# One-hots of the edge sums from a device-memory table, and the bias row of both tiles written by VectorE

## What is computed

```python
edge_feat = jnp.concatenate([x[src], x[dst], edge_attr], axis=-1)
h = mish(edge_feat @ W1 + b1)
messages = mish(h @ W2 + b2)
agg = jax.ops.segment_sum(messages, dst, num_segments=x.shape[0])
```

## Time and profile before

| | |
|---|---|
| median of 3 runs | 1096.25 us (1095.99 to 1096.29) |
| the profiled execution | 1095.75 us |
| its span | 1093.9 us |
| granted TensorE clock, mean | 0.989 |

### The profile page before, as it was taken

The page is one execution under the profiler, slowest core; times in us unless marked ns, Lnnn a source line. Parts: engine busy times, 40 slices in busy tenths (PEclk is TensorE's granted clock), DMA queues, the critical chain, the costliest instruction groups (busy, mean ns, idle before and its releaser), DMA issues.

```text
span 1093.9 us, 18566 instructions
## 1 busy us (share of the span) xinstructions
PE 1037.2 (95%) x5633; PEld 873.0 (80%) x5634; DVE 864.4 (79%) x1500; ACT 886.2 (81%) x1081; POOL 717.4 (66%) x622
## 2 busy tenths in 40 slices
PE   3668999999999999999999999999999999999997
PEld 1226889998889878888888888888888888888796
DVE  7998536635526389999999999999999999999686
ACT  6985735624603699999999999999999999999584
POOL 6874448553255587777777777777777777760227
PEclk9969999999999999999999999999999999999999
DMA  2006962773165387776666676666666666661002
GB/s 106 9 1 151 173 217 93 247 228 116 71 227 119 86 187 161 161 166 136 139 143 146 136 142 145 139 139 138 148 139 138 143 147 134 140 135 39 1 1 95
DMA packets 82914, 141.63 MB, mean 129 GB/s; under 512 B 11115, under 2 KB 39020, under 8 KB 82742
## 3 DMA queue, kind: packets, MB, share of 16 engines
q0 software_dynamic: 38048, 87.58, 39.8%
q1 hardware_dynamic: 44822, 53.52, 15.3%
HBM read 115.42 MB, written 20.39 MB: 124 GB/s over the span
## 4 chain that ended last, share of the span: by engine, by line
PE 85%; DVE 7%; ACT 3%; issue 2%; POOL 1%; DVEq 1%; DMA 1%; ACTq 0%; POOLq 0%
PE banks L1124 12%; PE banks L1125 12%; PE banks L1129 12%; PE banks L1023 9%; PE banks L1156 7%; PE banks L1106 7%; PE banks L1099 6%; PE banks L1066 5%; PE banks L941 4%; PE banks L1087 4%; DVE edge_counts L1799 2%; PE banks L1219 2%; DVE key_onehot L1738 1%; PE banks L996 1%; PE banks L1122 1%
## 5 line engine op out<-in xcount | busy, mean ns | idle before, releaser
L774 POOL DMA_INDIRECT gather_pq<-q_table,dst x157 | 325.2, 2071 | 57.1 <-issue 47.5
L766 POOL DMA_INDIRECT gather_pq<-p_table,src x157 | 174.9, 1114 | 118.6 <-PE banks L1106 67.6
L1124 PE MATMUL banks<-w_lo,h_hi 128*128 128x512 f32 x620 | 242.0, 390 | 0.0
L1125 PE MATMUL banks<-w_hi,h_hi 128*128 128x512 f32 x620 | 241.7, 390 | 0.0
L1129 PE MATMUL banks<-w_hi,h_lo 128*128 128x512 f32 x620 | 166.1, 390 | 0.0
L1129 PEld LDWEIGHTS banks<-w_hi,h_lo 128*128 128x128 f32 x620 | 116.4, 188 | 24.4
L1125 PEld LDWEIGHTS banks<-w_hi,h_hi 128*128 128x128 f32 x620 | 116.4, 188 | 23.7
L1124 PEld LDWEIGHTS banks<-w_lo,h_hi 128*128 128x128 f32 x620 | 116.4, 188 | 23.5 <-issue 0.8
L2107 DVE SCALAR_TENSOR_TENSOR h_full<-mish_work,banks 128x512 f32<-128x512 f32 (+1 forms) x154 | 98.4, 680 | 45.0 <-ACT mish_work L1443 41.2
L2132 DVE SCALAR_TENSOR_TENSOR message<-mish_work,banks 128x1024 f32<-128x1024 f32 x78 | 95.3, 1221 | 8.4 <-ACT mish_work L1467 0.3
L1099 PE MATMUL banks<-ident,gather_pq 128*128 128x128 f32 x628 | 96.5, 275 | 1.5 <-DVE h_full L2107 0.9
(11 more groups left out here) (268 smaller groups left out, 2610.6 us busy)
## 6 DMA issues: line engine op xcount, KB each, us to landing
edge_attr<-in_edge_attr_t SPq DMA_DIRECT2D x20, 256.0 KB, 2.9
attr_high<-edge_attr_hi SPq DMA_DIRECT2D x40, 128.0 KB, 2.1
attr_low<-edge_attr_lo SPq DMA_DIRECT2D x40, 128.0 KB, 1.8
edge_attr_parts<-attr_high SPq DMA_DIRECT2D x79, 64.0 KB, 2.8
edge_attr_parts<-attr_low SPq DMA_DIRECT2D x79, 64.0 KB, 3.7
x_nodes<-h_hi POOLq DMA_DIRECT2D x10, 256.0 KB, 15.0
x_nodes<-h_lo POOLq DMA_DIRECT2D x10, 256.0 KB, 7.8
p_table<-p_stage SPq DMA_DIRECT2D x10, 256.0 KB, 2.0
```

The source lines that it names most:

```text
L766: nc.gpsimd.indirect_dma_start(GP[:, 2 * j + k, :], None, p_tab[:, :], bass.IndirectOffsetOnAxis(ap=SRC[:, 2 * s + k:2 * s + k + 1], axis= ...
L774: nc.gpsimd.indirect_dma_start(GP[:, 2 * j + k, :], None, q_tab[:, :], bass.IndirectOffsetOnAxis(ap=DST[:, 2 * s + k:2 * s + k + 1], axis= ...
L1124: pe.matmul(at, h_high(s, j)[:, c, e], W2_LO[:, c, :], start=False, stop=False, skip_group_check=True)
L1125: pe.matmul(at, h_high(s, j)[:, c, e], W2_HI[:, c, :], start=False, stop=False, skip_group_check=True)
```

## The change

- The one-hots of the sums are no longer made in the loop. `four_hots` on DVE makes those of four edge tiles (one 128x512 comparison) in places ahead of the loop: 22 between the statistics of the first product, 7 in those of the second, 10 behind the rows of Q; `store_hots` on ACT issues a 256 KB store of each into a table in device memory. The two buffers lie in the unused part of `iota`, and POOL writes that part anew before the loop.
- In the loop SP loads the one-hots of one step at a time (128 KB), behind the attributes of a later step (`further_hots`), and PE waits for them ahead of the sums.
- DVE writes the bias row of both tiles with one copy (`b2_both_tiles`) behind each message. ACT's copy and PE's matmul with ones are gone for all steps from the third on.

```diff
+HOTS_BEHIND = 6
+HOT_PIECES_1 = [(o, b) for o in range(KH) for b in range(3) if b != 1 or o in (0, 1, 4, 5, 6, 7)]
+HOT_PIECES_2 = [(o, b) for o in range(KD) for b in (0, 2) if (o, b) != (KD - 1, 2)]
+HOT_GROUPS = -(-FINAL // 2)
...
+            def hots(q, j):
+                sp.dma_start(ONEHOT[:, j, :, :].rearrange("p k e -> p (k e)").bitcast(F32),
+                             hot_tab[bass.ds(q, 1), :, :].rearrange("o p e -> (o p) e")).then_inc(hots_in[j], 16)
+
+            def further_hots(q, j):
+                sp.wait_ge(seg_done, q - 1)
+                hots(q, j)
...
                 for j in range(SLOTS):
                     further_attributes(SLOTS * i + j, j)
+                    further_hots(SLOTS * i + j - HOTS_BEHIND, j % 2)
...
+            for j in range(2):
+                pool.wait_ge(hots_stored[j], 16 * ((HOT_GROUPS + 1 - j) // 2))
+            nc.gpsimd.iota(IOTA[:, P:NP], [[1, NP - P]], base=P, channel_multiplier=0,
+                           allow_small_or_imprecise_dtypes=True).then_inc(pool_const, 1)
...
-                if after(s, 2) and k == 0:
-                    pe.wait_ge(b2_first, s - 1)
-                elif after(s, 2) and j == 0:
-                    pe.wait_ge(b2_second, s)
+                if after(s, 2):
+                    if k == 0:
+                        pe.wait_ge(b2_seeded, s - 1)
                 else:
                     pe.matmul(at, ONES_R[:, :], B2_R[:, :], start=True, stop=False, skip_group_check=True)
...
+                else:
+                    pe.wait_ge(hots_in[j], 16 * (group + 1))
...
+            def store_hots():
+
+                g = hots_sent[0]
+                hots_sent[0] += 1
+                act.wait_ge(hots_made, g + 1)
+                nc.scalar.dma_start(hot_tab[2 * g:2 * g + 2, :, :].rearrange("q p e -> p q e"),
+                                    HOTS4[:, g % 2, :, :].rearrange("p (q k) e -> p q (k e)", q=2)).then_inc(hots_stored[g % 2], 16)
...
+                        if (o, b - 1) in pieces:
+                            store_hots()
...
-                if j == 1 and after(s, 3) and live(s - 1) and tiles(s - 1) == 2:
-                    b2_second_tile(s - 1, 1 - j)
...
+            def four_hots():
+
+                g = hots_begun[0]
+                hots_begun[0] += 1
+                if g >= 2:
+                    dve.wait_ge(hots_stored[g % 2], 16 * (g // 2))
+                wide = [P, GROUP, P]
+                nc.vector.tensor_tensor(HOTS4[:, g % 2, :, :], IOTA[:, 0:P].rearrange("p (o k) -> p o k", o=1).broadcast_to(wide),
+                                        REL_G[:, GROUP * g:GROUP * (g + 1)].rearrange("p (t o) -> p t o", o=1).broadcast_to(wide),
+                                        ALU.is_equal).then_inc(hots_made, 1)
...
+                        if (o, b) in pieces:
+                            four_hots()
...
-            def hots1(s, j):
-
-                make_hots([ONEHOT[:, j, k, :] for k in range(2)], REL_G, 2 * s).then_inc(hot_ready, 1)
-
...
-            def b2_first_tile(s, j):
+            def b2_both_tiles(s, j):
                 dve.wait_ge(msg_full, s - 1)
-                nc.vector.tensor_copy(Z2[:, 2 * j, :], B2_ROW[:, 0, :]).then_inc(b2_first, 1)
+                nc.vector.tensor_copy(Z2[:, 2 * j:2 * j + 2, :], B2_ROW[:, :, :].broadcast_to([P, 2, DIM])).then_inc(b2_seeded, 1)
...
-                if live(s - 2):
-                    hots1(s - 2, j)
-                    if live(s):
-                        b2_first_tile(s, j)
+                if live(s - 2) and live(s):
+                    b2_both_tiles(s, j)
```

More of the change, by code:

```diff
@@ L394, in gnn_kernel @@
         gat1 = [sem(f"gathered1_{j}") for j in range(SLOTS)]
-        hot_ready, seg_done, agg_done = sem("hot_ready"), sem("seg_done"), sem("agg_done")
+        seg_done, agg_done = sem("seg_done"), sem("agg_done")
+        hots_made, hots_stored, hots_in = sem("hots_made"), [sem(f"hots_stored{j}") for j in range(2)], [sem(f"hots_in{j}") for j in range(2)]
         last_hots = sem("last_hots")
@@ L577, in further_attributes, with w3_parts @@
                 attributes(s, j)
+            for j in range(2):
+                sp.wait_ge(hots_stored[j], 16 * ((HOT_GROUPS + 1 - j) // 2))
+            for q in range(2):
+                hots(q, q)
+            def w3_parts(c):
+                for part, table in ((W3_HI, w3_tabs[0]), (W3_LO, w3_tabs[1])):
+                    sp.dma_start(part[:, 0, bass.ds(c, 1), :].rearrange("p o n -> p (o n)").bitcast(F32),
+                                 table[bass.ds(c * P, P), :]).then_inc(w3_in, 16)
             sp.wait_ge(mm_done, MM_U)
-            with sp.Fori(1, 1 + KD) as i:
+            for s in range(SLOTS, 2 * SLOTS):
+                further_attributes(s, s - SLOTS)
+            w3_parts(0)
+            with sp.Fori(2, 1 + KD) as i:
                 for j in range(SLOTS):
                     further_attributes(SLOTS * i + j, j)
-                for part, table in ((W3_HI, w3_tabs[0]), (W3_LO, w3_tabs[1])):
-                    sp.dma_start(part[:, 0, bass.ds(i - 1, 1), :].rearrange("p o n -> p (o n)").bitcast(F32),
-                                 table[bass.ds((i - 1) * P, P), :]).then_inc(w3_in, 16)
+                    further_hots(SLOTS * i + j - HOTS_BEHIND, j % 2)
+                w3_parts(i - 1)
             with sp.Fori(1 + KD, EDGE_PAIRS // SLOTS) as i:
@@ L1135, in _, with segment1 @@
             FINAL_ROWS = [FINAL_MSG.rearrange("p c e -> p (c e)")]
-            def segment1(s, j, last):
+            def segment1(s, j, last, group):
                 final = isinstance(s, int) and s == FINAL
@@ L1175, in edge_step @@
                 if live(s - 4):
-                    segment1(s - 4, j, j == 1 or isinstance(s, int) and s - 4 == EDGE_PAIRS - 1)
+                    segment1(s - 4, j, j == 1 or isinstance(s, int) and s - 4 == EDGE_PAIRS - 1, group)
                 if live(s - 1):
@@ L1425, in _ @@
             nc.scalar.preload_act_table_set("natural_log_exp_and_others")
+            for _ in range(HOT_TABLE):
+                store_hots()
+            assert hots_sent[0] == HOT_GROUPS
             def exp1(s):
@@ L2194, in _ @@
                 edge_step(s, s % 2, s // 2)
+            dve.wait_ge(pool_const, 9)
             edge_step(3, 1, 1)
```

33 lines of the change are left out of this document (22 added, 11 removed).

## The result

The changed kernel takes 1137.8 us (median of 4 runs, 1135.2 to 1139.9) against 1096.3 before: ratio 1.037, 95% interval 1.0355 to 1.0386. That is slower, as forecast, but by 41.6 us instead of 14, and outside the range of 1095 to 1118.

A forecast was written before the change was run, and what follows sets the result against it. A ring of waits through DVE, ACT and PE was taken to bound the loop. 1095.75 + 12.6 (loop) + 1.6 (first product) + 0.3 (Q table) - 0.4 (drain) = 1109.85, or 1110.3 on the median's level; range 1095 to 1118.

The forecast's parts named there:

- The ring: Loop: chain of waits through DVE, ACT and PE sets the double step, 16.75 us before the change, 17.09 after.
- segment B: Loop: from the even step's full1 through PE and ACT to DVE's next full1, 7.92 us, unchanged by the change.
- rival (1): Loop: the wide bias-row copy is cheap, 0.70 us, so the loop gains 6.3 us and time is 1091.4; chance 0.13.
- The wait's price: Loop, DVE: the wide bias-row copy waits for message's semaphore and starts 0.11 us after message's end.
- rival (2): Loop: the semaphore wait costs nothing, the wide copy starts 1.14 after message; +5.6 us in all, 1103.3; chance 0.10.
- The +0.34: Loop, DVE: message to h_lo grows from 2.13 to 2.47 us per step; 37 double steps make 12.6 us.
- A: Loop: DVE's stretch from the odd step's full1 to the even step's, growing from 8.83 to 9.17 us.
- Rival (6): Loop: a transfer disturbs the gathers, 1115 us and more; chance 0.05, of it 0.02 above 1118.
- +1.6: First product: the last groups' wait for a store delays hidden_hi by 1.6 us (0 to 3).
- +0.3: Q stage: one more store lies beside the last Q table store, costing 0.3 us (0 to 2).
- Rival (5): Ahead of the loop: ACT issues of 1 us, landings of 4 us, at three places, +5 to +8: 1116; chance 0.10.
- Rival (3): Loop: PE is the bound after all, period near 16.5 us, -8.5 us, 1089 in all; chance 0.05.

The follow-up runs named there:

- range_only: Kernel before with only DVE's register load moved behind the odd step's message: 1093.2 us, ratio 0.996.
- gathers_later: Changed kernel with POOL clearing two tiles, and waiting for that, ahead of each step's P gathers: 1122.5 us, ratio 1.024.
- copy_in_eight: Kernel before with DVE's 512-column bias-row copy written as eight copies of 64 columns: 1116.8 us, ratio 1.019.
- no_stores: Changed kernel without the first 37 of 39 one-hot table stores and DVE's waits for them: 1123.8 us, ratio 1.024.

## Why the prediction was right in sign and wrong in size

**What bounds the kernel.** The ring through DVE, ACT and PE was read rightly in the main, segment B too (7.92; it stays 7.93). But "DVE works without a pause (the 0.26 ahead of the sums is issue)" took a wait for work. The first sum waits for PE's message sums, the last of which is this one:

```profile
616.49 0.39 PE L1156 MATMUL banks<-message_lo,onehot 128*128 128x512 f32 x1
```

It ends at 616.88, and the sum on DVE starts at 617.22, 0.34 later; that distance is 0.34 or 0.35 in every even step from 440 to 980 us. For DVE it was slack: the wide seed went into it, and after the change the sum follows h_lo at once. And the 1.50 from the first sum to full1 was taken as two sums. The two take 1.33 (range_only); the rest was the register load, whose end full1 waited for. A row of DVE's that is not counted as busy was on the path already, and "full1 at 618.72 starts the moment the sums are through" read it away.

**The seed.** 1.22 was right (1.23), which settles rival (1). The wait's price was 0.03 and not 0.11, between the forecast and rival (2). The +0.34 became +0.27 in message to h_lo and, with the slack, an estimated -0.06 in A with a fast load: 3.73 + 2.39 + 1.15 + 1.50 = 8.77 against 8.83. gathers_later has that A at a median of 8.82 against 8.81. The sum's largest term, 12.6 us, was thus near zero, and the 24.4 came from a coincidence that it set off. That the loop became slower, as forecast, was luck.

**The step that failed in the loop** is the one that moved instructions on DVE and asked only which DVE, ACT and PE rows follow. POOL was judged by its idle time: "POOL's gathers have 0.79 idle in front of them at 613.26. I cost the transfers at 0; if their cover went, it would be PE's transposes that wait for a gather." From 420 to 1040 us they never wait for one; POOL has more idle time after than before. But the gather's phase against h_lo changed by 0.25 us, and through it the load's length, from 0.75 to 1.62 us: that, and not the seed, made the loop's 24.4. Rival (6), "a transfer disturbs the loop's gathers", had a gather in it with the roles the wrong way round, and at 0.05.

**The step that failed ahead of the loop** is "In the first product PE sets the pace with four banks in hand, and all but the last groups are hidden", and with it "a 256 KB store lands in 2.0". That row is of stores in a calm stage; here the buffer came back after 7.7, and four banks hold only 7 us of work (a column of four blocks is done in 6.9, 55.55 / 8). The wait of the third group for the first one's store was seen, but costed only behind the last column. Expected +1.6, measured +13.6. In the Q stage, +0.3 expected and 5 measured: the comparison was costed at 0.75 wherever it stands, and one of them waited for a store and then stood beside POOL's subtractions. Rival (5) named the mechanism, with landings of 4 us and +5 to +8.

**The other terms.** Second product 0 and POOL's iota 0: right. The drain behind the loop changed by 0.1 and not by -0.4. Rival (3), PE as the bound at 16.5, did not come true in the changed kernel. With the register load off the path PE is the bound at 16.63 where it keeps its bias product, near the prediction's own 16.67; where it is freed of it, the 16.44 was not reached (16.62).

## What to carry to other kernels

Before shifting work on one engine, list what its queue does between the timed rows: this register load took 0.75 us at best, held all that was behind it, and belonged where its engine still had work in hand; moving it was worth 4 us here, and the whole change nothing. Where two engines share something, a change of 0.1 to 0.3 us in their phase can flip who comes first, so ask of each moved operation what starts beside it, not only who waits for it. And cost the return of a buffer by the busiest stage in which it is used, since a late store stops three engines if its wait and its issue stand in their queues ahead of the main work.

## What the runs showed of the hardware

- A register load of three words from SBUF takes 743 to 755 ns in the loop before, and 1043 to 1781 in the loop after, where a gather issued by GpSimd begins 0.1 to 0.3 us behind its start; in copy_in_eight a gather that begins up to 0.1 ahead of it does the same. Now and then such a gather does no harm (0.78 and 0.82 in no_stores). Gathers that began 0.45 us or more behind the load (gathers_later, before) left it alone. So did one that had begun 1.8 to 1.9 ahead and was still running (the fast loads of copy_in_eight): it is the gather's beginning that counts. Without the table's transfers the load was still 1.49. One load of the kernel before, at 399.3, took 1.45 with the nearest gather 0.36 ahead of it; that one is unexplained.
- A Q gather that begins 0.02 to 0.23 us inside VectorE's 128x1024 subtraction of two SBUF tiles takes 2.43 to 2.65 us instead of 1.57 to 1.60. The subtraction is not lengthened by a gather that begins ahead of it (1.21 to 1.27).
- A VectorE comparison of 0.68 us with both operands in SBUF took 5.71 beside four GpSimd subtractions and ended 0.56 behind the last of them; an addition with one operand in PSUM took 0.69 there.
- A 256 KB store to device memory gave its buffer back 7.7 us after its issue while weights were loaded (DMA share 0.8), against 2.0 in a calm stage.
- After 3.14 us without a matmul the granted TensorE clock was 0.50 (1.2 GHz) from 165 to 170 us, against 1.00 from 155 to 160.
